# Work shifted between engines at four places of a two-layer attention and feed-forward kernel, with the quantised input rows of the first feed-forward transposed by DMA

## The reference

```python
x = x + _L0_xattn_ref(_layernorm(x), ..., ctx_2048, ctx_2048, wq, wk, wv, wo)
x = x + _L0_ffn_ref(_layernorm(x), gate_w, gate_b, val_w, val_b, out_w, out_b)
x = x + _L1_xattn_ref(_layernorm(x), ctx_2048, mask, Wq, bq, Wk, bk, Wv, bv, Wo, qn_w, kn_w)
x = x + _L1_ffn_ref(_layernorm(x), router_w, gate_w, up_w, down_w, ...)
```

```python
def bit_linear(x, w, b):
    gamma_x = jnp.clip(jnp.max(jnp.abs(x), axis=-1, keepdims=True), 1e-05, None)
    scale_x = 127.0 / gamma_x
    x_dq = jnp.clip(jnp.round(x * scale_x), -128.0, 127.0) / scale_x
    gamma_w = jnp.clip(jnp.mean(jnp.abs(w)), 1e-05, None)
    w_dq = jnp.clip(jnp.round(w / gamma_w), -1.0, 1.0) * gamma_w
    return jnp.einsum('bsd,hd->bsh', x_dq, w_dq) + b
gate = jax.nn.silu(bit_linear(x, gate_w, gate_b))
val = bit_linear(x, val_w, val_b)
return bit_linear(gate * val, out_w, out_b)
```

## Time and profile before

| | us |
|---|---|
| median of 3 runs | 1839.73 (1837.72 to 1841.14) |
| the profiled execution, its own time | 1840.23 |
| its span, first to last instruction | 1838.5 |
| PE busy | 1745.0 (95%) |
| DVE busy | 1228.2 (67%) |
| ACT busy | 851.2 (46%) |
| POOL busy | 578.7 (31%) |

### The profile page before, as it was taken

How to read it: one execution, slowest core, us unless ns; L and a number is a source line. 1 busy time by engine, 2 the same in 40 slices (tenths; PEclk the granted TensorE clock), 3 DMA queues, 4 the chain that set the end, 5 groups by cost and what they waited for, 6 DMA issues and landing times. The chain is left out here.

```text
span 1838.5 us, 26726 instructions
## 1 busy us (share of the span) xinstructions
PE 1745.0 (95%) x9946; PEld 1447.7 (79%) x9966; DVE 1228.2 (67%) x2334; ACT 851.2 (46%) x1621; POOL 578.7 (31%) x413
## 2 busy tenths in 40 slices
PE   6999998985999889999999999999889999999999
PEld 6998997872444478888888888888767799999876
DVE  4444442996788757777677777777566567676655
ACT  3433432654555555554455555544331256566411
POOL 3111143325566621212121221211120246455342
PEclk9999999997999989999999999999889999999999
DMA  8223211852233562212122321110062388888573
GB/s 308 92 81 104 69 48 66 300 178 86 44 83 89 139 203 102 81 58 81 58 81 71 119 80 65 58 58 1 7 255 76 118 268 285 273 274 261 206 246 109
DMA packets 165434, 238.12 MB, mean 130 GB/s; under 512 B 42038, under 2 KB 101686, under 8 KB 163126
## 3 DMA queue, kind: packets, MB, share of 16 engines
q1 hardware_dynamic: 155420, 202.09, 33.7%
q0 software_dynamic: 9888, 34.35, 5.8%
HBM read 184.24 MB, written 43.78 MB: 124 GB/s over the span
## 5 line engine op out<-in xcount | busy, mean ns | idle before, releaser
L1173 POOL TENSOR_TENSOR a_rq<-a_ssq,a_qhalf 128x4 f32<-128x4 f32 x64 | 65.2, 1018 | 405.1 <-DVE a_ssq L1479 405.1
L1320 ACT ACTIVATE a_pT_hi<-bank 128x512 fp32r<-128x512 f32 x128 | 69.6, 598 | 186.6 <-PE bank L1709 186.6
L78 PE MATMUL bank<-a_xT_hi,a_wq_lo 128*128 128x512 f32 (+1 forms) x384 | 144.1, 375 | 9.4 <-issue 5.7
L1314 ACT ACTIVATE a_scores<-a_scores,a_nmax 128x256 f32<-128x256 f32 x256 | 127.2, 502 | 26.8 <-DVE a_nmax L1494 26.7
L80 PE MATMUL bank<-a_xT_hi,a_wq_hi 128*128 128x512 f32 (+1 forms) x384 | 139.0, 362 | 0.0
L79 PE MATMUL bank<-a_xT_lo,a_wq_hi 128*128 128x512 f32 (+1 forms) x384 | 138.0, 359 | 0.0
L78 PE MATMUL bank<-a_wo_hi,a_oT_lo 128*128 128x512 f32 x320 | 126.9, 397 | 2.9 <-DVE a_oT_lo L534 1.3
L2018 POOL TENSOR_TENSOR e_wg_lo<-raw_g,e_wg_hi 128x1408 fp32r<-128x1408 f32 x26 | 91.2, 3509 | 112.9 <-ACT e_wg_hi L2085 112.8
L79 PE MATMUL bank<-a_wo_lo,a_oT_hi 128*128 128x512 f32 x320 | 125.1, 391 | 0.0
L1487 DVE SCALAR_TENSOR_TENSOR a_scores<-bank,a_rq,a_mask 128x256 f32<-128x256 f32 x256 | 106.2, 477 | 28.3 <-PE bank L80 20.6
L80 PE MATMUL bank<-a_wo_hi,a_oT_hi 128*128 128x512 f32 x320 | 124.9, 390 | 0.0
(11 more groups left out here) (417 smaller groups left out, 5342.5 us busy)
## 6 DMA issues: line engine op xcount, KB each, us to landing
raw_g<-in_egw SPq DMA_DIRECT2D x26, 704.0 KB, 4.6
raw_u<-in_euw SPq DMA_DIRECT2D x26, 704.0 KB, 6.1
a_xT_hi<-x1T_hi SPq DMA_DIRECT2D x16, 1024.0 KB, 6.0
a_xT_lo<-x1T_lo SPq DMA_DIRECT2D x16, 1024.0 KB, 8.6
raw_d<-in_edw SPq DMA_DIRECT2D x26, 512.0 KB, 5.8
y_routed<-m_y SPq DMA_DIRECT2D x39, 256.0 KB, 6.2
raw_d<-in_edw SPq DMA_DIRECT2D x26, 192.0 KB, 6.3
a_cTraw<-in_ctxT SPq DMA_DIRECT2D x8, 512.0 KB, 5.8
```

The costliest lines, as they stand in the source:

```text
L78: pe.matmul(out, w[1], x[0], start=first, stop=False)
L1173: pool.tensor_tensor(rq[:, h % HG, :], ssq[:, h % HG, :], qhalf[:], ALU.pow).then_inc(s_rq, 1)
L1314: act.activation(row, row, ACT.Exp, bias=nmax[:, i % 2, t:t + 1], accum_out=den[:, i % 2, t:t + 1]).then_inc(s_exp, 1)
L1320: act.activation(pT[b].hi[:], ptb[b][:].rearrange("p (k s) -> p k s", k=QT), ACT.Copy).then_inc(ft.hi, 1)
```

## The change

- The first query weights are loaded in two halves and split in four blocks of 128 columns, of which two come ahead of the transposed rows on ACT and one on DVE; PE's first queries wait block by block.
- Stage 2: the pieces of weights are rounded one piece earlier (one in turn 0 and one in turn 12), `norm` moves from turn 13 to 12 and `largest` from 14 to 13, `keys_out(T - 2)` goes behind both `round_x`, and the last store moves from POOL to SP, with a semaphore of its own.
- Feed-forward: SP transposes `xq` by DMA (`rows_transposed`), three tiles ahead of the one in hand; PE keeps one small transpose per turn, of `r6`, and ACT one small copy. The scales' first two instructions stay on DVE, and move ahead to right behind `largest`; the other nine go to POOL, in turn 4g+2. The three splits move from turn 1 to turns 5 to 7 (ACT) and 6 to 8 (POOL), one in each. `fob` gets a second bank.
- `chunk(0)` goes where `xn` lies, and is issued two `hidden_transposed` earlier than the end, when all rows are quantised. The queries `q`, their squares and the second `K` buffer go where `wg` lies.

```diff
+    def query_weights(b):                       # ACT
+        act.wait_ge(s_wq[b // 2], 16)
+        act.activation(wq.hi[:, :, cols], wraw[0][:, :, cols], ACT.Copy).then_inc(s_wqhi, 1)
...
-            weights(0)
+            query_weights(0)
+            query_weights(1)
             transposed_x(0)
+            query_weights(2)
+            query_weights(3)
             weights(1)
...
-        rounded = {t: range(2 * t - 2, 2 * t) for t in range(1, PIECES // 2 + 1)}
+        rounded = {t: range(max(2 * t - 1, 0), min(2 * t + 1, PIECES)) for t in range(PIECES // 2 + 1)}
...
-                if t == T - 3:
+                if t == T - 4:
                     dve.wait_ge(s_rstd, 1)
                     for j in range(PREP):
                         norm(j)
+                if t == T - 3:
+                    largest()
                 if t == T - 2:
-                    largest()
                     scales()
...
+            def rows_transposed(t):
+                after(sp, s_xq, t + 1 - READY)
+                after(sp, s_v, (t - 2) * NH)
+                sp.dma_start_transpose(xqT[t % 3][:], xq[t % 2][:]).then_inc(s_xT[t % 2], 16)
...
-                if t == T - 1:
-                    sp.wait_ge(s_v, T * NH)
+                if t == T - 2:
+                    sp.wait_ge(s_xq, T - READY)
                     for j in range(2):
                         sp.wait_ge(s_x1st[j], CT // 2 * 32)
                     chunk(0)
                 hidden_transposed(t)
+                if t + 3 < T:
+                    rows_transposed(t + 3)
...
-                if n == 1:
-                    for k, (pair, raw) in enumerate(first.splits):
-                        pool.wait_ge(s_fhi, k + 1)
-                        pool.tensor_tensor(pair.lo[:], raw, f32(pair.hi[:]), ALU.subtract).then_inc(s_flo, 1)
+                if 6 <= n < 6 + len(first.splits):
+                    pair, raw = first.splits[n - 6]
+                    pool.wait_ge(s_fhi, n - 5)
+                    pool.tensor_tensor(pair.lo[:], raw, f32(pair.hi[:]), ALU.subtract).then_inc(s_flo, 1)
...
-                act.activation(rT[t % 3][0:NR, :], xb[0:NR, D:D + P], ACT.Copy)
-                act.activation(xqT[t % 3][:], xb[:, 0:D].rearrange("p (k s) -> p k s", k=KD), ACT.Copy).then_inc(s_xTc, 1)
+                act.activation(rT[t % 3][0:NR, :], xb[0:NR, 0:P], ACT.Copy).then_inc(s_rTc, 1)
...
             def down(t):
                 pe.wait_ge(s_hT, t * 16 + 16)
-                after(pe, s_fadded, t)
+                after(pe, s_fadded, t - 1)
```

More of the change, by code:

```diff
@@ L239, in attention0 @@
         s_w = [sem(f"w{j}_loaded") for j in range(4)]
+        s_wq = [sem(f"wq_half{j}_loaded") for j in range(2)]
+        s_wqhi, s_wqlo = sem("wq_hi_written"), sem("wq_lo_written")
         s_whi = sem("w_hi_written")
@@ L557, in _ @@
             norm(0)
-            weights(0)
+            query_weights(0)
             transposed_x(0)
+            for b in range(1, 4):
+                query_weights(b)
             weights(1)
@@ L1023, in ffn0_attention1 @@
         sc = [over.take(f"a1_scores{j}", [P, CT, S]) for j in range(2)]
+        over.offset += 4 * XS * D
+        V = [first.V, over.pair("a1_V", [P, CT, HD])]
+        over = Region(nc, keep.slab)
         q = [over.pair(f"a1_q{j}", [P, C]) for j in range(2)]
@@ L1026, in ffn0_attention1 @@
         K = [first.K, over.pair("a1_K", [P, C])]
-        V = [first.V, over.pair("a1_V", [P, CT, HD])]
+        assert over.offset <= keep.slab + 2 * KD * H
         over = Region(nc, prep.end)
@@ L1540, in _ @@
                     largest(g)
+                    scales(g)
                 if n >= 5:
@@ L1557, in _ @@
                     norm(GROUPS[g][0] + 3)
-                if ahead_of and i == 1:
-                    scales(g)
                 largest_half(n, 1)
@@ L1614, in _, with r_transposed @@
         def _(pe):
-            def x_transposed(t):
-                after(pe, s_xq, t + 1 - READY)
-                after(pe, s_xTc, t)
-                for c in range(KD):
-                    last = pe.transpose(xb[:, c * P:(c + 1) * P], xq[t % 2][:, c * P:(c + 1) * P], identb[:])
-                last.then_inc(s_xT, 1)
-                after(pe, s_rp, group(t) * 5)
-                pe.transpose(xb[0:NR, D:D + P], r6[:, t, :], identb[:]).then_inc(s_rT, 1)
+            def r_transposed(t):
+                after(pe, s_rTc, t)
+                after(pe, s_rp, group(t) * 7)
+                pe.transpose(xb[0:NR, 0:P], r6[:, t, :], identb[:]).then_inc(s_rT, 1)
             def next_xT(t):
@@ L1647, in down @@
                 pe.wait_ge(s_hT, t * 16 + 16)
-                after(pe, s_fadded, t)
+                after(pe, s_fadded, t - 1)
                 for c in range(KH):
-                    last = pe.matmul(fob[:], hqT[t % 2][:, c, :], fwo[:, c, :], start=c == 0, stop=c == KH - 1)
+                    last = pe.matmul(fob[t % 2][:], hqT[t % 2][:, c, :], fwo[:, c, :], start=c == 0, stop=c == KH - 1)
                 last.then_inc(s_fout, 1)
@@ L2750, in program @@
                                                       place(name + "_lo", shape, F32R, n * size // 3 + size // 6))
-            xT = [next_pair(f"a1_xT{j}", [P, KD, C], j) for j in range(2)]
             wq1 = next_pair("a1_wq1", [P, KD, HG * P], 2)
```

135 lines of the change are left out of this document (84 added, 51 removed).

## The result

The changed kernel takes 1820.9 us, the median of four runs (1819.24 to 1821.23), beside 1840.4 for the kernel before on the same chip: a ratio of 0.9891, 95% interval 0.9872 to 0.9909. The forecast was 1812 with a range of 1805 to 1825. The direction was right and the time is in the range, but 19.5 us were gained and not 28.2. The time is also 0.9 above the 1805 to 1820 that the forecast gave its likeliest case, in which all five terms are near their size.

What follows compares the result with a forecast made beforehand. PE, busy for 95% of the span, was taken as the bound. Terms of 2.4, 2.7, 8.0, 6.5 and 8.6 us summed to 28.2 off the profiled 1840.23, giving 1812 us, range 1805 to 1825.

Steps and rivals of the forecast that it cites:

- likeliest case: Whole kernel, first rival: the forecast holds with all five terms near their size, 1805 to 1820; chance 0.72.
- Start: Program start: only quarters of the weight splits stand ahead of the rows, first product at 12.3; 2.4 us gained.
- Border: Border of stages 2 and 3: earlier `kf`, one `keys_out` off the way, last store by SP; 2.7 us gained.
- so `kf` starts at 410.03, 2.3 earlier: Border of stages 2 and 3: moving `largest` a turn ahead lets DVE's last `kf` start 2.3 us earlier.
- SP's two issues take about POOL's time: Border of stages 2 and 3: moving the last store to SP was taken to cost about what POOL's issue did.
- Turns 0 to 2: First feed-forward turns: scales leave DVE and POOL's split leaves turn 1; 8.0 us gained, range 5 to 10.
- Later turns: Feed-forward from turn 3: PE's transposes and DVE's scales go, POOL's additions charged; 6.5 us gained, range 3 to 9.
- Seven turns have PE without DVE waits: 7 x 0.31 = 2.2: Turns from 3 on: seven turns without DVE waits each save PE's 0.31 us of transposes, 2.2 us.
- Both turns come down to PE's 23.66: Turns 5 and 6: without the scales on DVE, both together fall to 23.66 us, saving 3.2; turns 9 and 10 likewise.
- I charge 2.1 for both POOL additions: Later turns: nine scales and the 4.52 us split on POOL, mostly under `down` and slack, cost 2.1 us.
- The second rival: POOL's split holds DVE in turn 6 instead of turn 1; gain only 16.5 us, time 1824; chance 0.17.
- End: Feed-forward's end: second bank and earlier chunk remove PE's waits before `down(15)`; 8.6 us gained, range 6.5 to 9.

Runs made afterwards that it cites:

- old order: The changed kernel, but stage 2's roundings, norms, largest and ACT's last key rows stand at their old places; last store stays in SP's queue: 1820.3 us, 0.9889.
- the split in turn 1: The changed kernel, but with the three splits back in turn 1, scales still on POOL: 1825.6 us, ratio 0.9913.
- the scales on DVE: The changed kernel, but eight of a group's ten scale instructions are back on DVE, at the end of the group's second turn: 1823.8 us, ratio 0.9916.
- late splits: The changed kernel, but with the three splits (ACT's hi, POOL's lo) in turns 10 to 13 instead of 5 to 8: 1820.4 us, ratio 0.9893.
- the rows by PE: The changed kernel, but the first feed-forward's quantised rows are transposed by PE and copied by ACT, without DMA transposes of rows: 1813.0 us, ratio 0.9863.
- The late chunk: The changed kernel, but the next attention's first chunk is loaded at its old place, ahead of the last hidden tile: 1828.3 us, ratio 0.9937.
- The ghost transposes: Kernel with PE's row transposes, splits in turns 10 to 13, Wo loaded behind the last hidden tile; sixteen unread DMA row transposes added: 1815.3 us, 0.9859.

## Why the prediction was right, and where it was wrong

The direction came as forecast, and so did three of the five terms with their reasons: the start, turns 0 to 2 and the end. That the time lies in the range is in part luck: one term came at a fifth of its size, 2.6 us were given back at a place with no term, and a term with a wrong reason happened to come out larger than forecast.

**Start (2.4; 1.9 came).** Right in kind. The first product was put at 12.3 and came at 12.78, 1.41 us behind the transposes, which themselves ended 0.4 later than before. More than half of it came with the half loads and the blocks (1.2); the forecast named the half load only in passing.

**Border (2.7; 3.4 came).** Near in size by luck, for a wrong reason. The step "so `kf` starts at 410.03, 2.3 earlier" failed. DVE is busy for 80.7 of the 90 us from 326 to 416 in the kernel before, so moving `largest` ahead made the value rows late there (PE waits 3.0 us on them, 1.6 before), though its last wait, for the squares, fell from 5.57 to 3.50. Stage 2, from its first product for the squares to the last issue, takes 94.2 instead of 93.8, and 94.9 with the old order. What came is the store: "SP's two issues take about POOL's time" looked at the issues and not at the 4.96 us that lay behind POOL's. That was a visible idle gap of the rows before, which I read as the barrier's fixed price. That the whole stretch gained 3.4 as well is partly chance: with the scatter above, one pair of profiles does not tell it.

**Turns 0 to 2 (8.0; 7.5 came).** Right. Either half alone brings much of it back: the split in turn 1 6.1 us, the scales on DVE 3.7. They overlap, as the sum is above the 7.9 that both give together in turns 1 and 2. The DMA transpose at the start cost PE a 2.93 us wait, yet by turn 2's end the changed kernel is only 0.5 behind the one with PE's transposes.

**Later turns (6.5; 1.4 came).** This is the mis-sized term, 5.1 of the 9.2 us that are missing from 28.2 to the profiles' 19.0.

| turn | 5 | 6 | 7 | 8 | 9 | 10 | 11 | 12 | 13 |
|---|---|---|---|---|---|---|---|---|---|
| before | 12.71 | 14.17 | 12.14 | 12.14 | 13.21 | 14.17 | 12.14 | 12.13 | 12.14 |
| after | 11.91 | 13.16 | 12.13 | 13.58 | 13.20 | 13.39 | 12.14 | 11.91 | 11.92 |
| late splits | 11.92 | 13.14 | 12.13 | 11.91 | 12.49 | 13.39 | 12.17 | 11.91 | 12.87 |

Three steps of it failed. "Seven turns have PE without DVE waits: 7 x 0.31 = 2.2": a turn that PE bounds got 0.22 shorter, only turns 4, 12 and 13 got it in full, and the run with PE's transposes prices the whole at 0.4. "Both turns come down to PE's 23.66": turns 5 and 6 came to 25.07, turns 9 and 10 to 26.59, together 4.3 over. "I charge 2.1 for both POOL additions", hidden under slack: the splits cost turns 8 and 9 2.4 (nothing with the scales on DVE, where the same splits leave these turns at 11.92 and 12.50, so the price looks like that of both additions together), though turns 11 to 13 would have charged 1.0 for them.

I counted DVE's and POOL's instructions singly and missed the loop. DVE makes `vv`, POOL the product, and DVE's in-order queue stands at the largest of the second half until that product is there, 1.2 to 1.4 us in every turn. Then come the scale of `h` and ACT's rounding, and the next `gs`, for which PE waits, stands behind the rounding. So what makes DVE late, its own norms and largest (2.28 us) or POOL's split, reaches PE at `gs`: one wait of 0.9 us in each of turns 6, 8, 9 and 10. In turns 6 and 10 it was there before the change as well, at 0.90.

POOL's scales in turns 6 and 10 are not what keeps these at 13.1 to 13.4. They begin when the `gs` that PE waits for has begun. With all rows by PE and the scales in the same place, both turns take 12.1 to 12.2, and the lateness of DVE shows a turn earlier, as a wait for `xq` (13.1 and 13.6 in turns 5 and 9). The scales do make DVE stand in the first half too, 1.40 and 1.41 us instead of 0.4 or nothing, and that costs 0.2 in each turn behind: turns 7 and 11 take 12.13 and 12.14, but 11.91 with the scales on DVE. No run changed ACT's order or DVE's norms and largest, so their shares are read from the rows and not tested.

The second rival (the hold moves) was thus half right: it happened, 3.07 for 1.23, but cost 1.4 net and not 11.7. The page "SBUF — State Buffer" of the Trainium skill, section "Who interferes with whom", has a DVE copy or scale in a two-port mode and a GpSimd instruction take turns, and likewise a DVE instruction with two inputs in SBUF and a GpSimd one that reads it. The runs agree with both: 3.07 beside 4.55 for the first, 4.40 beside 4.50 for a maximum of one column.

**End (8.6; 7.3 came).** Right in kind. With the last hidden tile landed in time the same stretch is 34.12, a gain of 8.8. The 1.5 between is that tile's landing of 6.90 us where I had 4.3: I called the queue free and left out Wo's load. The late chunk shows that the chunk is the largest part.

**Not in the forecast: 2.6 us given back behind stage 3.** The text named it as what would make it wrong. The five kernels in which PE transposes all the rows (with before) have a rest of 1183.3 to 1185.3, the nine others 1187.1 to 1191.4. Between the first and the last transposes of the router lie 42.1 to 42.5 us in the five and 44.7 to 45.8 in the nine. From before to after this stretch grew by 2.9, the parts ahead of it and behind it changed by -0.6 and 0.2.

Two things make it up. DVE waits there for a store of `xn` to land, 4.58 us in the changed kernel and 2.62 with the rows by PE. From the second group of four stores on, the first store of a group lands 6.2 us after its issue in one group and 7.9 to 8.2 in the next, by turns. In the nine the slow one is the third group, which DVE waits for (8.18 in the changed kernel); in the five the third lands in 6.2, and DVE waits for none of the slow ones. The difference of the landings, 1.96, is that of the waits. And behind the longer wait PE's granted clock falls to its lower level for a short stretch, in all nine and in none of the five. The lines are of the changed kernel and of the rows by PE, each of a window that begins 4 us behind the end of the wait (granted clock 0.57 and 1.00):

```profile
1346.00:1350.00 4.00, 3.53 (x11) 1.40 (x12) 1.33 (x3) 0.09 (x1) 0.00 (x0) 0.57 0.72 295
1338.00:1342.00 4.00, 3.50 (x20) 2.21 (x21) 1.70 (x4) 1.43 (x3) 0.00 (x0) 1.00 0.72 289
```

The ghost transposes, whose kernel is one of the five, rule out the DMA transposes by themselves. What decides which group lands slowly (another count of instructions on PE and ACT, for one) was not tried and stays open. So does how much of the 7.9 us between 1820.9 and 1813.0 is due to the rows.

Five kernels measured below the changed one, at 1813.0 to 1818.1; the rows by PE is the lowest, and its interval overlaps those of the others. The rows by DMA are the part of the change that did not pay: in stage 3 they cost 1.6 us, and the longer rest goes with them in every kernel but the one with ghost transposes, where PE makes the rows as well.

## What to carry to other kernels

Where two engines hand work back and forth in order, price an addition by the round trip: each stand of the one for the other is part of its load, and work given to the partner comes back as a longer stand. Then follow the late work to the engine that bounds the time, and look at what began first: a cause that starts when the wait is nearly over is not its cause. Moving work ahead within a stage whose engine is busy for nine tenths moves the delay and not the end. And read the gap behind a barrier's last arrival by who issued last: it can be a queue's cost that moves with the instruction. Before a difference of a few us is put down to an edit, compare the granted clock in stretches whose code is the same.
